# Softmax denominators of an attention kernel: summed by VectorE instead of by TensorE

## The reference

```python
xn = _layernorm(x)
q, k, v = (xn @ W).reshape(b, s, 16, 64)            # for W in Wq, Wk, Wv
scores = einsum('bqhd,bkhd->bhqk', q, k) * 64 ** -0.5
out = einsum('bhqk,bkhd->bqhd', softmax(scores), v).reshape(b, s, 1024)
x = x + (out @ Wo + bo) + ffn(xn)                   # ffn: the expert with the largest router logit
```

## Time and profile before

| | us |
|---|---|
| median of three runs | 1388.52 (1387.92 to 1388.96) |
| the profiled execution, device time | 1389.63 |
| its span in the trace | 1387.9 |

### The profile page before, as it was taken

How to read it: one execution, slowest core, us unless ns; L and a number is a source line. 1 busy time by engine, 2 the same in 40 slices (tenths; PEclk the granted TensorE clock), 3 DMA queues, 4 the chain that set the end, 5 groups by cost and what they waited for, 6 DMA issues and landing times.

```text
span 1387.9 us, 20006 instructions
## 1 busy us (share of the span) xinstructions
PE 1365.8 (98%) x6447; PEld 866.1 (62%) x6447; DVE 1078.0 (78%) x1468; ACT 735.2 (53%) x1316; POOL 1121.8 (81%) x908
## 2 busy tenths in 40 slices
PE   7899999999999999999999999999999999999997
PEld 4566666566665666666766666656667666656644
DVE  7987887786787767777777777778677777788877
ACT  4465455565464554554644645545546446556543
POOL 7779997777787877877878877879777788789995
PEclk8999999999999999999999999999999999999998
DMA  4241113220132201331113311123112231111000
GB/s 104 58 120 41 37 41 70 70 67 20 43 89 57 60 19 43 94 69 44 34 39 84 73 40 43 43 71 90 24 42 55 64 79 26 24 23 33 11 19 23
DMA packets 65255, 72.38 MB, mean 52 GB/s; under 512 B 9024, under 2 KB 38272, under 8 KB 65152
## 3 DMA queue, kind: packets, MB, share of 16 engines
q1 hardware_dynamic: 64128, 69.01, 20.3%
q0 software_dynamic: 1024, 2.10, 0.5%
HBM read 17.83 MB, written 5.11 MB: 17 GB/s over the span
## 4 chain that ended last, share of the span: by engine, by line
PE 93%; DVE 2%; POOL 1%; DMA 1%; issue 1%; SPq 1%; ACT 1%; POOLq 0%; DVEq 0%; ACTq 0%
PE OB L1116 31%; PE SB L1062 17%; PE SB L1069 16%; PE MB L1088 15%; PE XB L1153 2%; PE XB L1144 2%; PE XB L1162 2%; PE XB L1050 1%; PE XB L1043 1%; POOL acc L505 1%; DVE mx L767 1%; PE XB L1123 1%; PE XB L1125 1%; PE XB L1124 1%; DMA K<-low 1%
## 5 line engine op out<-in xcount | busy, mean ns | idle before, releaser
L505 POOL TENSOR_TENSOR acc<-acc,ex 128x512 f32<-128x512 f32 x717 | 915.9, 1304 | 99.9 <-DVE acc L790 40.4
L767 DVE TENSOR_REDUCE mx<-MB 128x1 f32<-128x512 f32 x992 | 655.9, 688 | 228.9 <-PE MB L1088 224.1
L619 ACT ACTIVATE ex<-SB 128x512 f32<-128x512 f32 x1024 | 607.2, 599 | 329.8 <-PE SB L1069 262.0
L1116 PE MATMUL OB<-ex,V 128*64 128x512 f32 x2048 | 452.7, 594 | 0.0
L1062 PE MATMUL SB<-Q,K 128*128 128x512 f32 x1024 | 421.9, 412 | 0.5 <-ACT ex L619 0.5
L1069 PE MATMUL SB<-Q,K 128*128 128x512 f32 x1024 | 399.8, 390 | 0.8 <-DMA Q<-mrow 0.8
L1088 PE MATMUL MB<-K,Q 128*128 128x512 f32 x992 | 389.1, 392 | 1.6 <-DVE mx L773 0.6
L1116 PEld LDWEIGHTS OB<-ex,V 128*64 128x64 f32 x2048 | 143.9, 137 | 284.3 <-issue 273.0
L1062 PEld LDWEIGHTS SB<-Q,K 128*128 128x128 f32 x1024 | 192.6, 188 | 96.5 <-issue 53.5
L790 DVE TENSOR_TENSOR acc<-acc,ex 128x512 f32<-128x512 f32 x179 | 205.0, 1145 | 13.5 <-ACT ex L619 1.0
L1088 PEld LDWEIGHTS MB<-K,Q 128*128 128x128 f32 x992 | 186.1, 188 | 46.7 <-DVE mx L767 5.0
(11 more groups left out here) (136 smaller groups left out, 608.8 us busy)
## 6 DMA issues: line engine op xcount, KB each, us to landing
Q<-high SPq DMA_DIRECT2D x124, 128.0 KB, 2.3
K<-high SPq DMA_DIRECT2D x112, 128.0 KB, 2.3
Q<-low SPq DMA_DIRECT2D x64, 128.0 KB, 2.4
K<-low SPq DMA_DIRECT2D x56, 128.0 KB, 2.3
w<-fc SPq DMA_DIRECT2D x23, 256.0 KB, 2.7
w<-projT SPq DMA_DIRECT2D x23, 256.0 KB, 3.1
sorted_x<-res SPq DMA_DIRECT2D x1, 1472.0 KB, 6.9
tok<-sorted_x SPq DMA_DIRECT2D x23, 64.0 KB, 1.7
```

The source lines that it names most:

```text
L505: pool.tensor_tensor(a[:, :], src[:, :], EX[h][ex_slot(kt)][:, :], ALU.add).then_inc(done, 1)
L619: act.activation(EX[h][ex_slot(kt)][:, :], SB[bank_of(n, 2 * kt + h)][:, :], ACT.Exp).then_inc(a_e[h], 1)
L767: dve.tensor_reduce(mx[:, m % 2, u:u + 1], MB[bank_of(m, i)][:, :], AX.X, ALU.max).then_inc(v_m, 1)
L1116: mm = pe.matmul(OB[own[h], :], V[(n // JB) % 2][:, k, own[h]], EX[h][ex_slot(k)][:, :], start=(k == 0), stop=(k == NT - 1))
```

## The change

For blocks 0 to 30 PE's `denominators`, ACT's `take_sums` and DVE's `invert` are gone. In their place, for block n - 1 during block n:

- kt 0, DVE, behind its adds (`fold_sums`): for each head, `acc` (128x512) is transposed in squares of 32x32 into `turned` (the memory of `rd`), and the squares' columns are summed by a reduction over groups of 32. What is left are four partial sums for each denominator, one in each quarter of the partitions.
- kt 1 to 6, DVE, one small instruction each, behind the reductions of that kt (`sum_parts`): a copy of the upper 64 partitions to the lower ones, a sum, a copy of 32 partitions, a sum, the reciprocal, a 32x32 transpose. They have 64 or 32 partitions and 32 columns.
- SP: one transfer stores the 32x32 result to device memory (`store_row`), two spread it over `rd`'s 64 partitions of each head (`spread_rd`).
- POOL's `normalise` waits for these transfers instead of for the reciprocals.

```diff
+                def store_row(n):
+                    wait(sp, v_row, n.times(1, 1))
+                    wait(sp, d_rd, n.times(32))
+                    sp.dma_start(rows_rd.rearrange("h (t b) -> (h t) b", b=SQ), row[:, :]).then_inc(d_row, 16)
+                def spread_rd(n):
+                    wait(sp, d_row, n.times(16, 16))
+                    for h in range(2):
+                        sp.dma_start(rd[own[h], :], rows_rd[h:h + 1, :].to_broadcast([DH, QB])).then_inc(d_rd, 16)
...
                     for kt in range(NT):
                         for m in q_jobs(n, kt):
                             spread_q(m)
+                    if n.off:
+                        store_row(n - 1)
+                        spread_rd(n - 1)
                     if spread[1]:
                         spread_k(*spread[1][1:])
...
                 def normalise(n):
-                    wait(pool, v_rd, n.times(2, 2))
+                    wait(pool, d_rd, n.times(32, 32))
...
-                def take_sums(n):
-                    wait(act, t_den, n.times(1, 1))
-                    act.activation(rd[:, :], XB[:, :], ACT.Copy).then_inc(a_den, 1)
...
-                def invert(n, part):
-                    cols = slice(part * QB // 2, (part + 1) * QB // 2)
-                    wait(dve, a_den, n.times(1, 1))
-                    dve.reciprocal(rd[:, cols], rd[:, cols]).then_inc(v_rd, 1)
+                def fold_sums(n):
+                    for h in range(2):
+                        wait(dve, sums[h][n % 2], added(n, NT - 1))
+                        if h == 0:
+                            wait(dve, g_on, n.times(1))
+                        else:
+                            wait(dve, v_part, n.times(2, 1))
+                        dve.transpose(turned[:, :], acc[h][n % 2][:, :]).then_inc(v_turn, 1)
+                        wait(dve, v_turn, n.times(2, h + 1))
+                        dve.tensor_reduce(part[:, h * QB // SQ:(h + 1) * QB // SQ], turned[:, :].rearrange("p (t k) -> p t k", k=SQ),
+                                          AX.X, ALU.add).then_inc(v_part, 1)
+                def sum_parts(n, kt):
+                    if kt == 1:
+                        wait(dve, v_part, n.times(2, 2))
+                        dve.tensor_copy(upper[:, :], part[2 * SQ:4 * SQ, :]).then_inc(v_upper, 1)
+                    if kt == 2:
+                        wait(dve, v_upper, n.times(1, 1))
+                        dve.tensor_tensor(half[:, :], part[0:2 * SQ, :], upper[:, :], ALU.add).then_inc(v_sum2, 1)
+                    if kt == 3:
+                        wait(dve, v_sum2, n.times(1, 1))
+                        dve.tensor_copy(third[:, :], half[SQ:2 * SQ, :]).then_inc(v_third, 1)
+                    if kt == 4:
+                        wait(dve, v_third, n.times(1, 1))
+                        dve.tensor_tensor(den[:, :], half[0:SQ, :], third[:, :], ALU.add).then_inc(v_den, 1)
+                    if kt == 5:
+                        wait(dve, v_den, n.times(1, 1))
+                        dve.reciprocal(inv[:, :], den[:, :]).then_inc(v_inv, 1)
+                    if kt == 6:
+                        wait(dve, v_inv, n.times(1, 1))
+                        wait(dve, d_row, n.times(16))
+                        dve.transpose(row[:, :], inv[:, :]).then_inc(v_row, 1)
...
                         add_own(n, kt)
-                        if kt == AT_INV and not start:
-                            invert(n - 1, 0)
-                            invert(n - 1, 1)
+                        if kt == AT_FOLD and not start:
+                            fold_sums(n - 1)
+                        if not start:
+                            sum_parts(n - 1, kt)
...
-                def denominators(n):
-                    take_spare(a_den, n.times(1, 1))
-                    for h in range(2):
-                        wait(pe, sums[h][n % 2], added(n, NT - 1))
-                    for h in range(2):
-                        mm = pe.matmul(XB[own[h], :], ones[:, 0:DH], acc[h][n % 2][:, :], start=True, stop=True)
-                    mm.then_inc(t_den, 1)
...
-                        if kt == AT_DEN and not start:
-                            denominators(n - 1)
```

More of the change, by code:

```diff
@@ L83, in address @@
     return value if isinstance(value, int) else eng.snap(value)
+SQ = 32
 LEAD = 8
@@ L90 @@
 QS = 3
-AT_DEN, AT_KV, AT_Q, AT_WO, AT_NM, AT_T = 8, (1, 9), 5, 13, 11, 12
-AT_INV, AT_ON = 8, 10
+AT_KV, AT_Q, AT_WO, AT_NM, AT_T = (1, 9), 5, 13, 11, 12
+AT_FOLD, AT_ON = 0, 10
 AT_TOK, AT_UP, AT_DOWN = 3, 4, 11
@@ L163, in layer @@
         osb, rd = sb("osb", [P, QB]), sb("rd", [P, QB])
+        turned = rd
+        spare = halves[:, :, :].rearrange("p t s -> p (t s)")
+        part, upper, half = (spare[0:r, k * SQ:(k + 1) * SQ] for k, r in enumerate((P, 2 * SQ, 2 * SQ)))
+        third, den, inv, row = (sb(n_, [SQ, SQ]) for n_ in ("third", "den", "inv", "row"))
+        rows_rd = nc.dram_tensor("rows_rd", (2, QB), F32, kind="Internal").ap()
         on = osb
@@ L174, in layer @@
             sem(f"t_{n}") for n in ("s", "m", "pv", "q", "k", "v", "den", "wo", "nm"))
-        a_e, a_o, a_q, a_k, a_w, a_v, a_nm, a_den = (
-            [sem("a_e0"), sem("a_e1")], *(sem(f"a_{n}") for n in ("o", "q", "k", "w", "v", "nm", "den")))
+        a_e, a_o, a_q, a_k, a_w, a_v, a_nm = (
+            [sem("a_e0"), sem("a_e1")], *(sem(f"a_{n}") for n in ("o", "q", "k", "w", "v", "nm")))
         v_m, v_nm, v_q, v_k, v_w, v_rd, v_y = (
@@ L203, in layer @@
         v_y0 = sem("v_y0")
+        v_turn, v_part, v_upper, v_sum2, v_third, v_den, v_inv, v_row, d_row, d_rd = (
+            sem(n_) for n_ in ("v_turn", "v_part", "v_upper", "v_sum2", "v_third", "v_den", "v_inv", "v_row", "d_row", "d_rd"))
         d_out = sem("d_out")
@@ L753, in one @@
                             high_q(m)
-                        if kt == AT_DEN and not (n.i is None and n.off == 0):
-                            take_sums(n - 1)
                         if kt == AT_T and before(n, NB - 1):
@@ L985, in sum_head @@
                                                  in1=y, op0=ALU.mult, op1=ALU.add).then_inc((v_y0, v_y)[h], 1)
-                    dve.wait_ge(t_den, NB)
+                    dve.wait_ge(t_den, 1)
                     dve.reciprocal(rd[:, 0:2 * TB], XB[:, 0:2 * TB]).then_inc(v_rd, 1)
-                    dve.wait_ge(v_rd, 2 * (NB - 1) + 1)
+                    dve.wait_ge(v_rd, 1)
                     sum_head(0, 0)
@@ L1248, in last @@
                     n = Lin(NB - 1)
-                    take_spare(v_rd, 2 * (NB - 1) + 1)
+                    take_spare(v_rd, 1)
                     for h in range(2):
```

## The result

The changed kernel took 1436.65 us in the median of four runs (1433.02 to 1440.73), the kernel before 1388.74 us beside it on the same chip: a ratio of 1.0327, 95% interval 1.0264 to 1.0390. The change makes the kernel 3.3% slower. The profiled execution took 1440.06 us (span 1438.3 us), 50.4 us over that of before and 3.4 us over its own median.

What follows compares the result with a forecast made beforehand. TensorE (PE), busy for 98% of the span, was taken to bound the kernel unless another engine holds it back. 1389.6 - 27.9 (denominators removed) + 55.2 (losses before kt 8) = 1416.9, as a median 1416 us; range 1366 to 1440.

Steps and rivals of the forecast that it cites:

- Removed from PE: Denominator matmuls leave PE's stream before PV at kt 8: 0.90 us a block, over 31 blocks 27.9 us.
- The fold: At kt 0 on DVE, two transposes and two reductions take 3.16 us and fit under PV with nothing over.
- the rival of a longer fold: Transposes of 1.22 us make DVE 1.06 us late at kt 1: 21 us more, 1437; chance 0.05 (over 1440).
- The four waits: At kt 1 to 4 both small copies and both sums on DVE wait for GpSimd's running add; chance 0.55 with lost races.
- the first rival: Small copies don't contend with GpSimd, only two waits are left: 1370, or 1361 if sums find gaps; chance 0.28.
- The walk: Kt 1 to 4: DVE misses GpSimd's gap by 0.07 us, so kt 2, 3 and 4 take 2.43 us each.
- a block like 17: Twelve blocks with K: PE's last maxima matmul before PV at kt 8 comes 2.3 us late, 27.6 us in all.
- one like 15: Eleven blocks where PE makes V at kt 1 and DVE has no low_k: loss 0.9 us each, 9.9 in all.
- The second rival: Races with GpSimd's adds lost in some blocks only; each won saves up to 1.25 us: 1375 to 1395, chance 0.12.
- The rows by DMA: One store and two spreads put the inverted row in place by about 786, GpSimd reads at 789.56: costed at nothing.
- Blocks 28 to 30 (2.9): Blocks with neither K, V nor expert work on PE lose 2.9 us each before kt 8, 8.7 us in all.
- Blocks 2, 3 and 27 (1.9): Blocks with V but no expert work, put between 15 and 28, lose 1.9 us each, 5.7 us in all.

Runs made afterwards that it cites:

- e3: Changed kernel with the two small copies on ACT, the two sums on GpSimd, reciprocal and small transpose one kt later: 1379.96 us, ratio 0.9937 to the kernel before.
- e9: e3 with owners' search at kt 8, query projection at kt 6, and in blocks 3, 29, 30 the fold's second half at kt 1: 1365.89 us, ratio 0.9833.
- e1: Kernel before, denominators still on PE, plus only the four small copies and sums at kt 1 to 4 on unused data: 1456.47 us, ratio 1.0503.
- e2: Kernel before plus four reciprocals of the same shapes at the same places, instead of the copies and sums: 1387.78 us, ratio 0.9995.
- e6: Changed kernel with the two small copies moved to ACT and the two sums left on DVE: 1387.35 us, ratio 0.9997 to the kernel before.
- e4: Changed kernel with the 16 indirect transfers of blocks 28 to 30 replaced by plain GpSimd subtractions: 1429.36 us, ratio 1.0296 to the kernel before.

## Why the prediction was right, and where it was off

The direction, the mechanism and the ordinary blocks came out as written; the time was 20.6 us too low (1416 against 1436.65), near the upper end of a wide range (1366 to 1440), above which two of the four executions lie: that the median is inside has some luck in it. By its steps:

- **Removed from PE, 0.90 us a block.** Right: e3 and e9 show 0.90 to 0.91 us in each block in which nothing waits.
- **The fold, 3.16 us.** Right within 0.2: from 785.75 to 788.72 in block 17, 2.97 us. The transposes take 0.71 us, so the rival of a longer fold falls; that its 1437 us is the time measured is chance. The fold is hidden in the ordinary blocks (e3), but for K's low part, which it made late in six blocks, some 6.5 us: the prediction had nothing for that.
- **The four waits.** Right: the four take 0.70 to 1.18 us in the mean, and in the ordinary blocks end with GpSimd's add; and the reciprocal and the small transpose don't wait. That the copies wait decided it against the first rival. e1 and e2, the same shapes with and without the wait, differ by 68.7 us.
- **The walk: three races lost by 0.07 us, 2.3 us in a block like 17, 0.9 in one like 15.** Right: they are lost by 0.06 us in block 17, its loss is 1.52 + 0.90 = 2.4 us, and that of the V blocks 0.94. In V blocks the sum of kt 2 loses no race, as its reductions come late; it waits 0.4 us and ends with the same add as in the walk. Each step took 2.45 to 2.51 us in both kinds, two adds of GpSimd, where the walk had 2.43. The second rival, races lost in some blocks only, falls: all blocks of a kind but two agree within 0.05 us, and those two (9 and 12) were 0.7 and 1.1 us longer than their kind before the change. The price of two waits in the first rival, 0.4 us in a block like 17, stays open: in e6 the second sum did not wait.
- **The rows by DMA, nothing.** Right: GpSimd waited 0.7 us once.
- **"Blocks 28 to 30 (2.9)" and "Blocks 2, 3 and 27 (1.9)".** This term was mis-sized. It holds for 27 and 28 (2.0 and 2.9). In 2, 3, 29 and 30 the losses were 6.7, 8.3, 9.3 and 9.5 us where 9.6 stood for the four: 24.2 us too few, which is the difference and a little more. Two statements, taken from block 17, were carried into blocks that differ from it: that GpSimd's last sum "is there at 760.65, before DVE needs it", and that DVE waits until "GpSimd's running instruction is over". Both failed where GpSimd had issued indirect transfers: it is 2 to 3 us late there, and lets DVE in only when it pauses. The first could be read before the run: in the kernel before, GpSimd is busy with transfers and adds until 1270.52, where DVE has ended its adds at 1266.80. Of the second there was at most a hint, one add of DVE that took 2.42 us. On top of that PE lost its pace, 0.68 us a unit, which the walk took for given: at 1.2 GHz it took almost twice that, up to 9.7 us of the 24.2.

The Trainium skill (SBUF — State Buffer, section Who interferes with whom) says that whoever issues first has the shared ports for the whole instruction and the other is blocked for that long, and that `tensor_reduce` is never blocked. In the ordinary blocks the traces agree, 1.22 to 1.29 us for a copy or sum that waits for a whole add and 0.68 us for a reduction in the mean. Behind an indirect transfer they don't: a copy waited for six instructions (7.48 us in e1), though one of them ended every 1.25 us. There the measurement decides.

Why the wait outlasts the instruction behind an indirect transfer was not found. The runs show where it happens and that moving the transfer moves it. Nor does a run separate the clock's share of the loss from the waits'.

## What to carry to other kernels

A tiny instruction that must wait for another engine costs what it waits for, not what it does: four instructions of 0.2 us cost 68 us in e1, and four of 0.33 us that don't wait cost nothing in e2. A walk through one block is good for the blocks that are like it; before summing, look for the blocks in which the neighbour does something else (transfers it issues, backlog at the boundary), and walk these by themselves. A cover takes waits up to some size: 0.3 to 0.5 us of waiting a block was free (e6), 2.8 to 3.4 us cost 0.9 to 2.4 us. So it can be enough to move a part of the work to engines with room; but look in the trace whether the rest still waits: a shift of 0.1 us decided that here. And a long stand of TensorE can cost more than its length: look at the granted clock behind it.

## What the runs showed of the hardware

- Behind an indirect transfer that GpSimd issues, a DVE instruction that has to wait for GpSimd waits until GpSimd stops for another reason: for four adds (4.68, 4.74 and 4.83 us) or six (7.48 us). Without the transfer, at the same backlog, it waits for one (1.04 to 1.26 us; e4).
- A copy from SBUF to SBUF of 32 fp32 columns takes 0.17 us alone and waits like a sum of two tensors; reciprocal, transpose and reduction were not seen to wait.
- Between first and last PV, TensorE's granted clock fell to 0.50 (1.2 GHz) only in blocks in which PE had stood still (1.85 us in block 29 of the changed kernel), for 3.41 to 10.24 us, and matmuls came every 0.43 us instead of 0.23. Not every such stand brought it: in e4 PE stood for 2.13 us in blocks 29 and 30, and the clock stayed at 1.00 (2.4 GHz).
- Small sums and copies elsewhere cost little: 64x32 on GpSimd 0.25 us (median), on ACT 0.23 us.
